# When VectorE takes the running maximum and the key-norm forms in a cross-attention kernel: the order of three jobs inside a step

## What is computed

```python
q = (x @ Wq).reshape(B, 56, 16, 128);  k = (ctx @ Wk).reshape(B, 1500, 16, 128)
q = q * rsqrt(mean(q*q) + eps) * gq;   k = k * rsqrt(mean(k*k) + eps) * gk
attn = softmax(q @ k.T / sqrt(128))
out  = attn @ v            # v = ctx @ Wv
```

## Time and profile before

| | |
|---|---|
| median of 3 runs | 1315.98 us (1315.48 to 1316.28) |
| the profiled execution | 1316.16 us; its span 1314.4 us, so 1.8 us lie around the span |
| busy, share of the span | PE 95%, DVE 89%, POOL 81%, ACT 74% |
| granted TensorE clock | 0.996 of full speed |

### The profile page before, as it was taken

One profiled execution on the slowest core, in us unless ns is written; L12 is line 12 of the kernel. 1 busy time (PEld: TensorE's weight loads), 2 busy tenths in 40 slices (PEclk: granted clock), 3 DMA queues, 4 the chain that ended last, 5 costly groups with the idle time before them and its releaser, 6 DMA issues.

```text
span 1314.4 us, 24031 instructions
## 1 busy us (share of the span) xinstructions
PE 1242.9 (95%) x6024; PEld 958.7 (73%) x6024; DVE 1170.7 (89%) x4434; ACT 971.3 (74%) x4019; POOL 1061.6 (81%) x937
## 2 busy tenths in 40 slices
PE   8889989999999999999999999999999999999998
PEld 5767656677777777777777777777777777778787
DVE  5865679999999999999999999999999999997655
ACT  2667886888888888888888888888888888863342
POOL 5744452889898989898989898989898989997740
PEclk9999999999999999999999999999999999999999
DMA  7050240101010101010101010101010101030300
GB/s 255 34 197 1 73 168 18 54 25 48 24 48 25 48 25 48 24 48 24 48 24 48 24 48 24 48 25 48 24 48 25 48 24 48 1 112 1 135 4 28
DMA packets 34106, 66.55 MB, mean 51 GB/s; under 512 B 3056, under 2 KB 22640, under 8 KB 32176
## 3 DMA queue, kind: packets, MB, share of 16 engines
q1 hardware_dynamic: 32976, 64.66, 14.8%
q10 hardware_dynamic: 992, 0.36, 0.1%
HBM read 56.89 MB, written 8.13 MB: 49 GB/s over the span
## 4 chain that ended last, share of the span: by engine, by line
POOL 45%; PE 31%; issue 15%; DVE 6%; ACT 2%; DMA 1%; POOLq 0%; ACTq 0%; DVEq 0%
POOL xa_den L1225 18%; POOL probs_r L1239 8%; POOL xa_scores L1214 6%; PE om_ps L1586 3%; PE xa_o_ps L1579 3%; POOL xa_ctx_m L1175 2%; POOL xa_den L1232 2%; POOL xa_q_lo L1149 2%; POOL xa_nat_r L1245 2%; PE xq_ps L636 2%; POOL ctxT_lo L1155 2%; PE xa_k_ps L1496 1%; DVE xa_k_ps L1393 1%; PE xa_k_ps L1485 1%; PE xa_s_ps L1485 1%
## 5 line engine op out<-in xcount | busy, mean ns | idle before, releaser
L1323 ACT ACTIVATE xa_k_ps<-xa_k_ps 125x128 f32<-125x128 f32 x1536 | 399.3, 260 | 61.9 <-PE xa_k_ps L1487 59.7
L1393 DVE CUSTOM_DVE_ANT_0 xa_k_ps<-xa_k_ps,xa_ctx_m 125x128 f32<-125x128 f32 x1536 | 399.1, 323 | 16.7 <-PE xa_k_ps L1497 14.5
L1323 ACT ACTIVATION_READ_ACCUMULATOR xa_k_ps<-xa_k_ps 125x1 f32 x1536 | 283.7, 185 | 0.0
L1225 POOL TENSOR_TENSOR xa_den<-probs,xa_den 125x896 f32<-125x896 f32 x128 | 271.6, 2122 | 5.8 <-ACT probs L1306 5.8
L1408 DVE TENSOR_TENSOR xa_scores<-xa_s_ps,xa_rk 125x448 f32<-125x448 f32 x384 | 238.1, 620 | 11.1 <-PE xa_s_ps L1487 11.0
L1496 PE MATMUL xa_k_ps<-wk_parts,xa_ctxT_hi 128*125 128x512 f32 x384 | 208.1, 542 | 34.3 <-ACT xa_k_ps L1323 30.0
L1306 ACT ACTIVATE probs<-xa_scores 125x896 f32<-125x896 f32 x192 | 181.7, 946 | 71.4 <-issue 45.7
L1393 DVE DVE_READ_ACCUMULATOR2_ANT xa_ss<- 125x1 f32 x1536 | 218.7, 142 | 0.0
L1422 DVE TENSOR_TENSOR xa_max_ps<-xa_scores,xa_max_ps 125x448 f32<-125x448 f32 x320 | 200.9, 628 | 9.9
L1239 POOL TENSOR_TENSOR probs_r<-probs,xa_p_hi 125x896 fp32r<-125x896 f32 (+1 forms) x96 | 197.7, 2059 | 0.6
L1579 PE MATMUL xa_o_ps<-probs,xa_ctx_nat 125*128 125x448 f32 x396 | 181.5, 539 | 0.0
(11 more groups left out here) (193 smaller groups left out, 2615.2 us busy)
## 6 DMA issues: line engine op xcount, KB each, us to landing
xa_ctx_m<-in_ctx SPq DMA_DIRECT2D x48, 250.0 KB
xa_ctx_nat<-in_ctx SPq DMA_DIRECT2D x16, 750.0 KB
ctxT_in<-in_ctxT SPq DMA_DIRECT2D x84, 125.0 KB, 2.1
qo<-in_xo_w SPq DMA_DIRECT2D x1, 2048.0 KB, 15.8
qo<-in_xq_w SPq DMA_DIRECT2D x1, 2048.0 KB, 16.1
vo_scratch<-qo SPq DMA_DIRECT2D x2, 1024.0 KB, 4.0
w_parts_scratch<-ws_hi SPq DMA_DIRECT2D x2, 1024.0 KB, 6.2
w_parts_scratch<-ws_lo SPq DMA_DIRECT2D x2, 1024.0 KB, 7.2
```

The costliest lines, as they stand in the source:

```text
L1225: pool.tensor_tensor(den2[:, :, :], probs_pair(y), so_far, ALU.add).then_inc(den_done, 1)
L1323: last = act.activation(cols, cols, ACT.Square, scale=MEAN ** 0.5, accum_out=ss[:, j // 2, head:head + 1])
L1393: form = dve.tensor_tensor_reduce(cols, cols, ctx_m[:, j // 2, :], 2 * MEAN, 0.0, ALU.mult, ALU.add, ss[:, j // 2, head:head + 1])
```

## The change

In a step that has all three jobs, VectorE did forms, scaling, maximum of this tile. It now does, at t of 1 and more, scaling, maximum of the tile before (from t = 2), forms. At t = 0 it does the last maximum of the half before, forms, the scaling twice. The reduction at t = 1 comes between scaling and forms; the small sum, the shifts and the three instructions of t = 9 still stand at the end of the step. The number and shapes of all instructions stay; no other engine's program is touched.

```diff
+            def take_forms(ph, j):
+                if j % (2 * MT) == 0:
+                    dve.wait_ge(m_ready, m_count(ph, j // (2 * MT)))
+                dve.wait_ge(k_done, ph.at(2 * STEPS, 2 * STEPS + 2 * j + 1))
+                for g in range(GH):
...
+                form.then_inc(formed, 1)
+
+            def running_max(ph, j):
+                h, t = divmod(j, KT)
+                dve.wait_ge(s_taken, pos_s(ph, j) + 1)
+                wait(dve, max_done, ph.at(2 * (KT - 1), (KT - 1) * h + t - 1))
+                if t == KT - 1:
+                    wait(dve, max_turned, ph.at(2, h))
+                dve.tensor_tensor(cmax[0:KP, :] if t == KT - 1 else max_ps[0:KP, 0:UW], score_slot(ph, j),
+                                  max_ps[0:KP, 0:UW], ALU.max).then_inc(max_done, 1)
...
-                    if ph.within(-1, 14):
-                        if j % (2 * MT) == 0:
-                            dve.wait_ge(m_ready, m_count(ph, j // (2 * MT)))
-                        dve.wait_ge(k_done, ph.at(2 * STEPS, 2 * STEPS + 2 * j + 1))
...
+                    if t == 0:
+                        if ended_half(ph, h):
+                            running_max(ph if h else ph.shift(-1), (j - 1) % STEPS)
+                        if ph.within(-1, 14):
+                            take_forms(ph, j)
                     if ph.within(0, 15):
...
+                    if ph.within(0, 15) and t >= 2:
+                        running_max(ph, j - 1)
                     if t == MAX_TURN and ended_half(ph, h):
...
-                    if ph.within(0, 15) and t >= 1:
-                        dve.wait_ge(s_taken, pos_s(ph, j) + 1)
-                        wait(dve, max_done, ph.at(2 * (KT - 1), (KT - 1) * h + t - 1))
...
+                    if ph.within(-1, 14) and t:
+                        take_forms(ph, j)
```

More of the change, by code:

```diff
@@ L1378, in _ @@
             link = linker(dve, mlp.dve_chain)
+            def take_forms(ph, j):
[3 more added lines that the diff above has]
+                for g in range(GH):
+                    cols = k_ps[0:KP, (2 * j) % 3, g * C:(g + 1) * C]
+                    head = UH * (j % 2) + g
+                    form = dve.tensor_tensor_reduce(cols, cols, ctx_m[:, j // 2, :], 2 * MEAN, 0.0, ALU.mult, ALU.add,
+                                                    ss[:, j // 2, head:head + 1])
+                form.then_inc(formed, 1)
[7 more added lines that the diff above has]
+                                  max_ps[0:KP, 0:UW], ALU.max).then_inc(max_done, 1)
             def body(ph):
```

## The result

The changed kernel takes **1343.14 us** (median of 4 runs, 1342.60 to 1343.68) beside 1316.13 us for the kernel before (4 runs, 1315.48 to 1316.71): ratio 1.0205, 95% interval 1.0188 to 1.0223. It is slower by 27 us. Forecast were 1338 us, with 1306 to 1360 as the range. The profiled execution took 1343.68 us, 27.5 more than the one before.

A forecast was written before the change was run, and what follows sets the result against it. VectorE was taken as the bound. Its 62.0 us a batch plus waits of 2 x 1.53 + 2.16 + 0.21 gave 67.4 against 65.66; fourteen phases add 24.8 us, phase 0 saves 2.4: 1338 us, range 1306 to 1360.

The forecast's parts named there:

- What sets the pace: Full phases: VectorE, busy 68.13 of 70 us, sets the pace; TensorE's scores are 1.2 us ahead at t = 3.
- rival (1): VectorE stays the bound and TensorE keeps its lead: 30 halves x 1.2 us = 36 us less, 1280 us; chance 0.08.
- The saving: Scaling to maximum on VectorE falls from 0.66 to 0.54 us for t = 2 to 11, 1.2 us a half.
- Rival (3): The 0.12 us is a price of the pair scaling and maximum, not a write wait; 1367 us; chance 0.04.
- Forms(10) to scaling(3): Into the next half: TensorE takes 11.43 us against VectorE's 9.90, so VectorE waits 1.53 us every half.
- t = 7: VectorE's scaling waits for TensorE's scores: 2.16 us in the odd half, 0.21 us in the even half.
- rival (2): Only the half's wait is real, the copy of t = 5 is absorbed: 8 us less, 1308; chance 0.20 with mixtures.
- The batch: Batch period, phases 1 to 14: 67.4 us against 65.66, +1.77 us each, +24.8 us in all.
- Phase 0: Few value products, TensorE busy only 44.20 of 50 us: it keeps its gain, 20 x 0.12 = 2.4 us.
- The late gate alone: TensorE's second key tile waits for forms, 0.30 us when gated; VectorE's scaling waits for scores at its queue's head.

The follow-up runs named there:

- e11: The kernel before the change with only the second `nat_hi` copy on ScalarE and its GpSimd subtraction one step later; 1315.22 us, ratio 0.9993.
- e5: The kernel before with the maximum one tile late, forms still first, the copy and subtraction a step later, value product ahead of second key tile; 1305.09 us.
- e6: The changed kernel with the copy and its subtraction a step later and the value product ahead of the second key tile; 1305.02 us, ratio 0.9923.
- e1: The kernel before with only the maximum taken one tile late, forms still at the head of the step; 1304.85 us, ratio 0.9909.
- e12: The kernel before, VectorE's order untouched, with the later copy, the value product ahead and ScalarE's rounding a step earlier; 1302.70 us, ratio 0.9909.
- e9: e5 with ScalarE's rounding of the next tiles' transposed values for step 12 done at the head of step 11; 1279.33 us, ratio 0.9720.
- e7: The changed kernel with forms put back to the front at t = 10 and 11 (t = 0 already so); 1329.56 us, ratio 1.0111.
- e3: The changed kernel with the second `nat_hi` copy on ScalarE and its GpSimd subtraction one step later; 1316.14 us, ratio 0.9998 to the kernel before.
- e2: The kernel before with only the forms moved behind scaling and maximum from t = 1, the maximum of the same tile; 1371.05 us, ratio 1.0415.
- e8: The kernel before, VectorE untouched, but TensorE's second key tile also waits for the maximum of the step before; 1343.47 us, ratio 1.0216.

## Why the prediction was right, point by point

- **What sets the pace.** That VectorE did, and that TensorE ran 1.2 us ahead at t = 3, holds: e11 shows the lead covering a wait that costs 27 us without it. Not seen was a third limit close by, although the chain with GpSimd at 45%, which the prediction set aside, pointed at that engine. GpSimd, with its stop for ScalarE, holds the batch of e5 and e6 at 65 us, 0.6 under the old period. e1, with TensorE's lead kept, gains 11.5 us and not the 36 of rival (1). The limit didn't touch the forecast only because the forecast lay on the slow side of it; that it was missed without harm is luck.
- **The saving.** 0.66 to 0.54 us from scaling to maximum: as predicted. Rival (3) is out. The Trainium skill, "VectorE: DVE Perf Modes", section "The DRAIN you can't avoid", lets the next VectorE instruction start only when the pipe is empty, but adds that one that isn't held starts earlier, which the prediction left out; the condition for it stands in the Trainium skill, same page, section "Two Vector instructions with no wait between them". The trace agrees with the exception: 0.54 us, where the row of the scaling is 0.62 long. What the saving is worth was shown between e12 and e9: 23.4 us of the 30 x 1.2 = 36 that all halves could give. Of the rest, 30 x 0.16 = 5 us are an estimate for the last two maxima of a half, which e9 has behind each other at 0.70 instead of 0.54 us; the remaining 8 are no more than what VectorE waits in e9 (12 us, 260 to 1150 us) and not in e12 (1 us).
- **Forms(10) to scaling(3).** Predicted 11.43 us on TensorE, against 9.90 on VectorE; measured 11.48. Right. e7 opened the gate earlier in this loop and got 13.6 us back. Second key tiles waited for the forms at many more steps than the t = 5 and 11 of the forecast, but the period shows that this cost little beyond the sum.
- **t = 7.** Odd half: predicted wait 2.16 us, measured 2.07 and 2.05. The chain second tile, value product, copy, squares, first tile was tested by e3, which moves only the copy and its subtraction and takes 27 us off. So rival (2), that the copy would be absorbed, is out; ScalarE's idle time before it grew from 2.67 to 3.26 us. In the even half 0.21 was predicted; the scaling comes 0.24 us late (606.99 instead of 605.80 + 0.95).
- **The batch.** Predicted 67.43 and +1.77 us. From the first scaling of phase 1 to that of phase 15 there are (1196.51 - 251.06) / 14 = 67.53 us; before, the same is 65.62. So +1.91, and 14 x 0.14 = 2 us of the miss lie here, 0.14 us in a sum of a dozen terms. VectorE's busy share in full phases is 64.72 of 70 us, 92%, as predicted.
- **Phase 0.** This is the term that was mis-sized: "it keeps its gain, 20 x 0.12 = 2.4 us". It gained nothing (56.33 for 56.12 us). The gain is there with forms first (53.85 in e1), and the late forms eat it up: TensorE was idle a lot in phase 0, but idle *for the forms* (second key tiles there waited 9.9 us for them before and 11.5 after), and from the forms to the scaling every other plain step takes 1.21 us (200.87 to 202.08) instead of 0.96 (203.15 to 204.11). The prediction had read TensorE's low busy share as slack. That is 2.6 us of the miss; with the batches' 2 and about 0.5 at both ends it makes the 5 us between 1338 and 1343.
- **The late gate alone.** The prediction named two things that the move does: TensorE starts the second tile later, and VectorE wants the scores at the head of its queue. e2 and e8 bear both out, at some 27 us each without the lag. My expectation for e8, made after the result, was 13 us too low; the 31.7 us in which its forms wait for the first key tile were under-priced in it.

## What to carry to other kernels

Two engines in step have a lead, and the order inside one's queue decides how much of it the other may use: before moving a job behind another, follow what the other engine has queued behind the wait for it, around the whole loop and back. A copy or a tile that costs nothing may do so only because of that lead, so try it again after each change of order. And when several different edits end at the same time to a microsecond, look for the engine that none of them touched; here moving one rounding of ScalarE took one of four kernels at 1305 us to 1279. And two variants with the same time need not have the same cause: set each beside the run that differs from it in one thing.

## What the runs showed of the hardware that was not expected

The start-to-start time of two VectorE instructions on 125x448 depends on whether the second reads what the first wrote: 0.54 us if not, 0.66 for a maximum behind its own scaling, and 0.70 for a maximum that reads the maximum in front of it. The first two were expected; the last was not, and is from e1, at the end of a half:

```profile
569.50 0.61 DVE L1399 TENSOR_TENSOR xa_max_ps<-xa_scores,xa_max_ps 125x448 f32<-125x448 f32 x1
570.20 0.62 DVE L1399 TENSOR_TENSOR xa_cmax<-xa_scores,xa_max_ps 125x448 f32<-125x448 f32 x1
570.74 0.29 DVE L1388 CUSTOM_DVE_ANT_0 xa_k_ps<-xa_k_ps,xa_ctx_m 125x128 f32<-125x128 f32 x1
```

The lengths of the rows (0.61 to 0.63 us) show nothing of this; only the starts do.
